# Decoder kernel, fp8 attention stage: the next x is transposed in another PSUM bank, and two norms stand one step later

## The chip, the cores and the metric

The kernel runs on one NeuronCore of a Trainium2 chip. The metric is the time on the device for one execution, in microseconds. Five engines run their own queues in order and meet at semaphores: TensorE (PE; PEld is its weight load), VectorE (DVE), ScalarE (ACT), GpSimd (POOL) and SyncE (SP), which issues the DMAs.

## The reference

A decoder of two layers over x of 16 sequences x 128 tokens x 256 channels. After each block the residual sum is layer-normed. The order is: linear attention, cross-attention, ternary MLP; then a state-space block, the fp8 attention, and a last ternary linear layer. Only the last two are touched here:

```
ln_out = ln(x) * ln_w + ln_b
q, k, v = fp8_linear(ln_out, ...)                # inputs rounded to fp8 values; q: 16 heads, k, v: 4 + 4 groups
q, k = ln(q), ln(k)                              # per head
core = softmax(q k^T / sqrt(d)) v
qx from ln_out; kx, vx from cond @ w_kv_x        # the same attention over the context
cat = fp8(clip([core, xout] / proj_smooth))
y = cat @ wproj * scale
x = layernorm(x + y)                             # norm of the attention, "norm" in the kernel
x = layernorm(x + ternary_linear(x))             # the last norm, "tnorm" in the kernel
```

There are 32 heads in all (16 of each attention) of 128 channels, handled four at a time: 8 units of one batch element.

## The kernel before, in words

The stage is `fp8_attention_and_linear`. Each engine has a function `steps(m, side, attend, front, back, last_linear)` that issues its work for one period m, written out by hand in eight steps j = 0 to 7. Nothing is planned by a scheduler: the order in these functions is the order on the engine. Steps are software-pipelined. In step j of period m:

- TensorE makes the scores of unit j+1 into bank pS (L1920), transposes the probabilities of unit j-1 into bank pP (L1928), multiplies unit j-2 with v into pO (L1938), adds unit j-4 to the projection pY (L1951), transposes the keys of the next batch element into bank pH (L1970), makes a key or value projection of the next element into pJB (L1901 from the context, L1881 from x), transposes the queries of unit j+2 into pH (L2002) and projects those of unit j+3 into pJA (L1881).
- ScalarE does the exponentials of unit j (L2037), copies pP to pT (L2043), copies the keys out of pH (L2028, kT) and the queries out of pH (L2028, qT), then takes the sums of squares of keys or copies v (L2021 k_junk, L2066), and the sums of squares of queries (L2021 q_junk).
- GpSimd turns each sum of squares into a reciprocal root (rs: L1834 and L1837), keys first, then queries, and does two additions of the fp8 rounding of the attention output (ov L1851, cat L1860), and powers for the norms (L107, L1864).
- VectorE takes the maxima of the scores (L2154), scales keys (kn, L2164) and queries (qn, L2170), normalises the probabilities (L2185), and rounds the outputs (L2198 to L2215) and the inputs x (L2129 to L2220, in steps 2 to 6). The norm of the attention has its sum and statistics in step 4 and its apply in step 5 (L112); the last norm has its statistics in step 5 (L98 to L103) and its apply in step 7 (L112).

Keys stand in steps 1, 2, 5 and 6 (`OTHERS`). In step 1 the x of the next batch element is turned too: VectorE makes xn (L2120), TensorE transposes it into pH (L1961), ScalarE scales it into lnT (L2047), and only then the key transposes may use pH. Periods m = 0 to 2 and 16 to 18 are written out singly, m = 4 to 15 are a loop with two periods in its body (`Fori(4, B - 1, 2)`). `attend` holds for m = 1 to 16, `front` (work for the next element) for m = 0 to 15, `back` for m = 2 to 17, `last_linear` for m = 3 to 18.

Of the kernel before, what the change touches and what calls it, by code (L numbers as in the profile page):

```python
# [22 lines left out]
ACT = mybir.ActivationFunctionType  # L23
# [1659 lines left out]
def fp8_attention_and_linear(nc, env, dram, out, ctx, spare):  # L1683
# [147 lines left out]
    def gpsimd(pool):  # L1831
        def rstd(sems, cols, j, count):
            pool.wait_ge(sems["squared"], count)
            pool.tensor_tensor(rs[:, j % 2, cols], ms[:, j % 2, cols], env.eps5w[:, cols], ALU.add)\  # L1834
                .then_inc(sems["eps"], 1)
            pool.wait_ge(sems["eps"], count)
            pool.tensor_tensor(rs[:, j % 2, cols], rs[:, j % 2, cols], env.mhalf[:, cols], ALU.pow)\  # L1837
                .then_inc(sems["rstd"], 1)

        def steps(m, side, attend, front, back, last_linear):  # L1840
            there = presence(attend, front, back)
            for j in range(UNITS):

                if front and j > 0 and OTHERS[j - 1][0] == "k":
                    rstd(kk, slice(HG, 2 * HG), j, at(m + 1, OTHERS[j - 1][1], 4))
                if there(j + 2):
                    rstd(q, slice(0, HG), j, at(m, j + 2))
                if there(j - 3):
                    i = (j - 3) % 2
                    pool.wait_ge(a["om"], at(m, j - 3))  # L1850
                    pool.tensor_tensor(ov[:, i], ob[:, i], om[:, i], ALU.add).then_inc(a["added"], 1)  # L1851
                if front and 2 < j < 7:
                    st = STREAMS[j - 3]
                    pool.wait_ge(sx["xm_done"], at(m + 1, j - 3, 4))
                    pool.tensor_tensor(xv[:, st], xb[:, st], xm[:, st], ALU.add).then_inc(sx["x_added"], 1)
                if attend and not back and j == 3:
                    pool.wait_ge(wp_low, UNITS)
                if there(j - 3):
                    pool.wait_ge(a["added"], at(m, j - 3))
                    pool.tensor_tensor(cat[:, 4 * ((j - 3) % UNITS):4 * ((j - 3) % UNITS) + 4, :], ov[:, i],  # L1860
                                       om[:, i], ALU.subtract).then_inc(a["cat"], 1)
                if front and j == 0:
                    pool.wait_ge(s["eps0_done"], at(m + 1, 0, 1))
                    pool.tensor_tensor(rs0[:], mv0[:, 1:2], env.mhalf[:, 0:1], ALU.pow)\  # L1864
                        .then_inc(s["rs0_done"], 1)
                if back and j == 4:
                    norm.pool_rstd(pool, m - 1, 0)
                if last_linear and j == 6:
                    tnorm.pool_rstd(pool, m - 2, 0)

        env.ssm_stage.left(pool)
        pool.wait_ge(env.fa_ready, 1)
        sequences(pool, steps)

    def tensor(pe):
# [33 lines left out]
        def steps(m, side, attend, front, back, last_linear):  # L1909
            there = presence(attend, front, back)  # L1910
            for j in range(UNITS):
# [12 lines left out]
                if there(j - 1):  # L1924
                    pe.wait_ge(a["p_done"], at(m, j - 1))
                    pe.wait_ge(a["pT_in"], at(m, j - 1) - 1)
                    for i in range(HG):
                        last = pe.transpose(pP[:, i * P:(i + 1) * P], pr[:, (j - 1) % 2, i, :], env.ident[:])  # L1928
                    last.then_inc(a["pT_ps"], 1)
# [24 lines left out]
                    if n == UNITS - 1:  # L1954
                        last.then_inc(s["y_ps"], 1)

                if front and j == 1:
                    pe.wait_ge(s["xn_done"], at(m + 1, 0, 1))
                    pe.wait_ge(q["T_in"], at(m, j + 1))
                    for k in range(KT):  # L1960
                        last = pe.transpose(pH[:, k * P:(k + 1) * P], xn[:, k * P:(k + 1) * P], env.ident[:])  # L1961
                    last.then_inc(s["xn_ps"], 1)
                if keys:
                    n = OTHERS[j - 1][1]
                    pe.wait_ge(kk["scaled"], at(m + 1, n, 4))
                    pe.wait_ge(q["T_in"], at(m, j + 1))
                    if j == 1:
                        pe.wait_ge(s["lnT_in"], at(m + 1, 0, 1))
                    for i in range(HG):
                        last = pe.transpose(pH[:, i * P:(i + 1) * P], kn[:, i, :], env.ident[:])  # L1970
                    last.then_inc(kk["T_ps"], 1)
# [16 lines left out]
                    last.then_inc(t["y_ps"], 1)  # L1988
                if front:
                    other(m + 1, 1 - side, *OTHERS[j])  # L1990
                if there(j + 2):
                    n = (j + 2) % UNITS
                    pe.wait_ge(q["scaled"], at(m, j + 2))
                    pe.wait_ge(q["T_in"], at(m, j + 1))
                    if keys:
                        pe.wait_ge(kk["T_in"], at(m + 1, OTHERS[j - 1][1], 4))
                    if last_linear and j == 3:
                        pe.wait_ge(t["xqT_in"], now(m - 2, 0))
                    if last_linear and j == 4:
                        pe.wait_ge(tnorm.summed, now(m - 2, 0))  # L2000
                    for i in range(HG):
                        last = pe.transpose(pH[:, i * P:(i + 1) * P], qn[:, n % 2, i, :], env.ident[:])  # L2002
                    last.then_inc(q["T_ps"], 1)
# [13 lines left out]
    def scalar(act):  # L2017
# [13 lines left out]
        def steps(m, side, attend, front, back, last_linear):  # L2031
            there = presence(attend, front, back)
            for j in range(UNITS):
                if there(j):
                    act.wait_ge(a["bias"], at(m, j))
                    for i in range(HG):
                        last = act.activation(four(pS[j % 2])[:, i, :], four(pS[j % 2])[:, i, :], ACT.Exp,  # L2037
                                              bias=nb[:, j % 2, i:i + 1],
                                              accum_out=rsum[:, j % 2, i:i + 1])
                    last.then_inc(a["exp"], 1)  # L2040
                if there(j - 1):
                    act.wait_ge(a["pT_ps"], at(m, j - 1))
                    act.activation(pT[:, (j - 1) % 2], four(pP), ACT.Copy).then_inc(a["pT_in"], 1)  # L2043
                if front and j == 1:
                    act.wait_ge(s["xn_ps"], at(m + 1, 0, 1))
                    for k in range(KT):
                        last = act.activation(lnT[:, k, :], pH[:, k * P:(k + 1) * P], ACT.Identity,  # L2047
                                              bias=vec[:, k, 1:2], scale=vec[:, k, 0:1])
                    last.then_inc(s["lnT_in"], 1)
                if front and j > 0 and OTHERS[j - 1][0] == "k":  # L2050
                    n = OTHERS[j - 1][1]
                    head_in(kk, kT[:, 1 - side, n // 2, 4 * (n % 2):4 * (n % 2) + 4, :],
                            6 if n < 2 else 2, m + 1, n, 4)
                if last_linear and j == 3:
                    act.wait_ge(t["xqT_ps"], now(m - 2, 0))
                    act.activation(txqT[:], pH[:, :].bitcast(BF16)[:, 0:D], ACT.Copy).then_inc(t["xqT_in"], 1)
                if there(j + 2):
                    n = (j + 2) % UNITS
                    head_in(q, qT[:, n % 2], 0 if n < 4 else 4, m, j + 2, UNITS)
                if front:  # L2060
                    kind, n = OTHERS[j]
                    if kind == "k":
                        square(kk, pJB, k_junk, ms[:, (j + 1) % 2, HG:2 * HG], m + 1, n, 4)
                    else:
                        act.wait_ge(v_ps, at(m + 1, n, 4))
                        act.activation(v[:, 1 - side, n // 2, (n % 2) * 512:(n % 2 + 1) * 512], pJB[:, :],  # L2066
                                       ACT.Copy).then_inc(v_in, 1)
                if not attend and front:
                    act.wait_ge(wp_in[j % 2], 16 * (j // 2 + 1))
                    act.activation(w_proj[:, 0, 4 * j:4 * j + 4, :], wp_raw[:, j % 2], ACT.Copy)\  # L2070
                        .then_inc(wp_high, 1)
                if there(j + 3):
                    square(q, pJA, q_junk, ms[:, (j + 1) % 2, 0:HG], m, j + 3, UNITS)
# [5 lines left out]
    def vector(dve):  # L2079
# [63 lines left out]
        def steps(m, side, attend, front, back, last_linear):  # L2143
            there = presence(attend, front, back)
            for j in range(UNITS):
# [76 lines left out]
                if not attend and front:  # L2222
                    dve.wait_ge(wp_high, j + 1)
                    dve.tensor_tensor(w_proj[:, 1, 4 * j:4 * j + 4, :], wp_raw[:, j % 2],
                                      w_proj[:, 0, 4 * j:4 * j + 4, :], ALU.subtract).then_inc(wp_low, 1)
                if back and j == 5:
                    norm.vector_apply(dve, m - 1, 0)
                if last_linear and j == 5:
                    tnorm.vector_stats(dve, m - 2, 0)
                if last_linear and j == 7:  # L2230
                    tnorm.vector_apply(dve, m - 2, 0)
# [201 lines left out]
```

## Time and profile before

| | |
|---|---|
| median of 3 runs | 2268.47 us (2267.84 to 2269.28) |
| the profiled execution | 2267.87 us, its span 2265.9 us, mean TensorE clock 0.971 of full speed |
| busy over the span | PE 2043.1 us (90%), DVE 1676.3 (74%), ACT 1332.4 (59%), POOL 1258.8 (56%) |
| chain that ended last | PE 62%, DVE 16%, ACT 10%, issue 7%, POOL 4% |
| periods m = 4 to 14 of this stage | 583.93 us for 11, from the xn transposes of one to those of the next, at full clock |

Busy time is an average over six stages. The stage of the change begins at about 1356 us. A period is found in the timeline by the transposes of xn (L1961), once in each. Times in the rows below are microseconds from the start of the span.

### The profile page before, as it was taken

The page shows a single profiled execution, that of the slowest core. Times are in us where ns is not written, and L with a number is a line of the kernel's source. Part 1 is how long each engine was busy: PE and PEld are TensorE (multiplying, and loading weights), DVE is VectorE, ACT ScalarE, POOL GpSimd, SP SyncE. Part 2 cuts the span into 40 slices and gives each one's busy share as a digit, 9 for nine tenths or more (in the row PEclk, how much of TensorE's full clock was granted, in tenths as well). Part 3 has the DMA queues.
Part 4 walks back from the last instruction along what each step waited for, and adds up shares of the span by engine and source line. Part 5 has one row for each costly group of instructions (what it writes and reads, how often), then busy time and mean ns, then how long its engine had stood idle before and what let it go on. Part 6 is the DMA issues. An engine that isn't in the chain of part 4 may idle for free.

```text
span 2265.9 us, 35512 instructions
## 1 busy us (share of the span) xinstructions
PE 2043.1 (90%) x10014; PEld 1339.2 (59%) x10116; DVE 1676.3 (74%) x3833; ACT 1332.4 (59%) x5022; POOL 1258.8 (56%) x1508
## 2 busy tenths in 40 slices
PE   7889999999999997888889875999999999999996
PEld 5546665666666665555555542666666666666664
DVE  7755676676666777888887864678888888877886
ACT  3655666666666665333333315777777777777773
POOL 0153444544444532566666652676767777776775
PEclk9989999999999999999999987999999999999998
DMA  6000000000000002000000002000000000000000
GB/s 216 1 19 3 3 4 2 5 2 2 2 2 5 0 32 114 1 19 19 19 19 10 1 24 58 4 3 6 6 9 5 6 5 6 5 5 8 3 3 8
DMA packets 30093, 37.61 MB, mean 17 GB/s; under 512 B 3328, under 2 KB 24320, under 8 KB 29312
## 3 DMA queue, kind: packets, MB, share of 16 engines
q1 hardware_dynamic: 29952, 36.11, 4.8%
q8 instruction: 42, 0.69, 0.1%
q14 instruction: 99, 0.81, 0.1%
HBM read 34.00 MB, written 2.10 MB: 16 GB/s over the span
## 4 chain that ended last, share of the span: by engine, by line
PE 62%; DVE 16%; ACT 10%; issue 7%; POOL 4%; DMA 0%; DVEq 0%; SPq 0%; POOLq 0%; ACTq 0%
PE xa_pJB L736 5%; PE xa_pS L755 5%; PE fa_pJB L1901 5%; PE xa_pO L829 5%; PE xa_pY L859 5%; PE xa_pJA L736 4%; PE fa_pS L1920 4%; PE ssm_pX L1404 3%; PE fa_pY L1951 3%; PE fa_pO L1938 3%; PE fa_pJA L1881 3%; PE ssm_pL L1398 3%; PE fa_pH L2002 2%; DVE ssm_y L1665 2%; PE fa_pJB L1881 2%
## 5 line engine op out<-in xcount | busy, mean ns | idle before, releaser
L1346 POOL TENSOR_TENSOR ssm_y<-ssm_y,ssm_term 128x512 f32<-128x512 f32 x112 | 141.9, 1267 | 129.5 <-DVE ssm_term L1612 127.4
L1837 POOL TENSOR_TENSOR fa_rs<-fa_rs,all_minus_half 128x4 f32<-128x4 f32 x192 | 198.2, 1032 | 15.1
L2028 ACT ACTIVATE fa_qT<-fa_pH,all_fa_head_vec 128x512 f32<-128x512 f32 x128 | 99.6, 778 | 173.6 <-PE fa_pH L2002 173.6
L2037 ACT ACTIVATE fa_pS<-fa_pS,fa_nb 128x128 f32<-128x128 f32 x512 | 183.1, 393 | 6.9 <-issue 6.5
L1834 POOL TENSOR_TENSOR fa_rs<-fa_ms,all_eps5w 128x4 f32<-128x4 f32 x192 | 43.7, 228 | 242.1 <-ACT fa_q_junk L2021 132.4
L1920 PEld LDWEIGHTS fa_pS<-fa_kT,fa_qT 128*128 128x128 f32 x1024 | 124.0, 191 | 65.3 <-ACT fa_qT L2028 58.4
L1398 PE MATMUL ssm_pL<-ssm_xd,ssm_cb 128*128 128x512 f32 x224 | 122.3, 643 | 44.3 <-DVE ssm_term L1612 40.5
L1860 POOL TENSOR_TENSOR fa_cat<-fa_ov,fa_om 128x512 bf16<-128x512 f32 x128 | 153.7, 1201 | 5.3
L682 POOL TENSOR_TENSOR xa_rs<-xa_ms,all_eps 128x4 f32<-128x4 f32 (+1 forms) x65 | 13.1, 202 | 258.1 <-ACT xa_junk L904 258.1
L1920 PE MATMUL fa_pS<-fa_kT,fa_qT 128*128 128x128 f32 x1024 | 148.1, 288 | 2.8 <-ACT fa_qT L2028 0.9
L1851 POOL TENSOR_TENSOR fa_ov<-fa_ob,fa_om 128x512 f32<-128x512 bf16 x128 | 147.8, 1154 | 4.7 <-DVE fa_om L2215 4.7
L755 PE MATMUL xa_pS<-all_shared_weights,xa_qT 128*128 128x256 f32 x512 | 125.8, 387 | 23.4 <-ACT all_shared_weights L935 17.5
L2170 DVE TENSOR_TENSOR fa_qn<-fa_pJA,fa_rs 128x512 f32<-128x512 f32 x128 | 88.5, 691 | 77.3 <-POOL fa_rs L1837 77.2
L920 ACT ACTIVATE xa_pr<-xa_pS,xa_nb,xa_rs 128x256 f32<-128x256 f32 x256 | 140.9, 566 | 0.2
L2154 DVE TENSOR_REDUCE fa_nb<-fa_pS 128x4 f32<-128x512 f32 x128 | 88.0, 688 | 69.5 <-PE fa_pS L1920 54.7
L1951 PE MATMUL fa_pY<-all_shared_weights,fa_cat 128*128 128x256 bf16 x1024 | 134.0, 274 | 4.0 <-POOL fa_cat L1860 4.0
L2021 ACT ACTIVATE fa_q_junk<-fa_pJA 128x128 bf16<-128x128 f32 x512 | 136.2, 301 | 0.4
L1404 PE MATMUL ssm_pX<-ssm_w_tap,ssm_xT 128*128 128x512 f32 x256 | 135.6, 647 | 0.0
L2037 ACT ACTIVATION_READ_ACCUMULATOR fa_pS<-fa_pS,fa_nb 128x1 f32 x512 | 133.3, 260 | 0.0
L1938 PE MATMUL fa_pO<-fa_pT,fa_v 128*128 128x256 f32 x512 | 131.9, 380 | 1.4 <-DVE fa_ob L2198 1.4
L1901 PE MATMUL fa_pJB<-all_shared_weights,fa_ctxT 128*128 128x512 f32 x256 | 127.7, 623 | 5.5 <-DMA fa_ctxT<-in_ctxT 4.8
L755 PEld LDWEIGHTS xa_pS<-all_shared_weights,xa_qT 128*128 128x128 f32 x512 | 93.1, 190 | 58.7 <-issue 41.1
(330 smaller groups left out, 5942.1 us busy)
## 6 DMA issues: line engine op xcount, KB each, us to landing
all_shared_weights<-in_fa_w SPq DMA_DIRECT2D x12, 512.0 KB, 3.7
fa_cat<-in_fa_wproj SPq DMA_DIRECT2D x8, 512.0 KB, 3.8
all_shared_weights<-in_xa_wq SPq DMA_DIRECT2D x1, 2048.0 KB, 13.8
xa_wo<-in_xa_wo SPq DMA_DIRECT2D x1, 2048.0 KB, 18.0
xa_ctxT<-in_ctxT SPq DMA_DIRECT2D x16, 128.0 KB, 2.1
all_shared_weights<-in_fa_wkvx SPq DMA_DIRECT2D x1, 2048.0 KB, 10.0
fa_ctxT<-in_ctxT SPq DMA_DIRECT2D x16, 128.0 KB, 2.1
out_x<-all_X SPq DMA_DIRECT2D x16, 128.0 KB, 1.7
```

What stands on the lines that cost most here:

```text
L736: last = pe.matmul(bank[:, :], lhs[k], w[:, k, at0:at0 + 512], start=(k == 0), stop=(k == KT - 1))
L755: last = pe.matmul(pS[b][:, (h % 2) * NK:(h % 2 + 1) * NK], qT[:, n % 2, h, :], kT[:, to, :, n, :], start=True, stop=True)
L1398: pe.matmul(pL[in_turn(side, l)][:, :], cb[:, side, l, :], xd[:, side, l, :], start=True, stop=True).then_inc(level_ps, 1)
L1404: return pe.matmul(pX[:, :], xT[:, k, t:t + P], w_tap[:, t, k, 0:HID], start=(n == 0), stop=(n == TAPS * KT - 1))
L1837: pool.tensor_tensor(rs[:, j % 2, cols], rs[:, j % 2, cols], env.mhalf[:, cols], ALU.pow)\
L1851: pool.tensor_tensor(ov[:, i], ob[:, i], om[:, i], ALU.add).then_inc(a["added"], 1)
L1860: pool.tensor_tensor(cat[:, 4 * ((j - 3) % UNITS):4 * ((j - 3) % UNITS) + 4, :], ov[:, i], om[:, i], ALU.subtract).then_inc(a["cat"], 1)
L1901: last = pe.matmul(pJB[:, :], ctxT[:, side, k, :], w_kvx[:, k, c * 512:(c + 1) * 512], start=(k == 0), stop=(k == KT - 1))
L1920: last = pe.matmul(pS[n % 2][:, i * P:(i + 1) * P], qT[:, n % 2, i, :], kT[:, to, 1 if n < 4 else 0, (4 * (n % 4) + i) // 2, :], start=Tru ...
L1938: last = pe.matmul(pO[:, 2 * i * P:(2 * i + 2) * P], v[:, to, 1 if n < 4 else 0, g * HD:(g + 1) * HD], pT[:, n % 2, 2 * i:2 * i + 2, :], s ...
L1951: last = pe.matmul(pY[:, 0:D], cat[:, hd, :], w_proj[:, part, hd, :], start=(n == 0 and i == 0), stop=(n == UNITS - 1 and i == 2 * HG - 1))
L2037: last = act.activation(four(pS[j % 2])[:, i, :], four(pS[j % 2])[:, i, :], ACT.Exp, bias=nb[:, j % 2, i:i + 1], accum_out=rsum[:, j % 2, ...
```

## The change

In step 1, the transposes of the next x move behind the key transposes and the projection L1901, and go into bank pP (that of the probabilities) instead of pH. ScalarE makes lnT from pP, now behind the copy of the queries. TensorE waits for lnT before the next transposes of the probabilities, in step 2. On VectorE, the apply of the attention's norm and the statistics of the last norm move from step 5 to step 6. On GpSimd, the power for the last norm moves from the end of step 6 into step 7, behind the queries' pair and ahead of ov and cat.

```diff
 gpsimd, steps:
                 if there(j + 2):
                     rstd(q, slice(0, HG), j, at(m, j + 2))
+                if last_linear and j == 7:
+                    tnorm.pool_rstd(pool, m - 2, 0)
...
                 if back and j == 4:
                     norm.pool_rstd(pool, m - 1, 0)
-                if last_linear and j == 6:
-                    tnorm.pool_rstd(pool, m - 2, 0)
 tensor, steps:
                     pe.wait_ge(a["pT_in"], at(m, j - 1) - 1)
+                    if front and j == 2:
+                        pe.wait_ge(s["lnT_in"], at(m + 1, 0, 1))
                     for i in range(HG):
                         last = pe.transpose(pP[:, i * P:(i + 1) * P], pr[:, (j - 1) % 2, i, :], env.ident[:])
...
-                if front and j == 1:
-                    pe.wait_ge(s["xn_done"], at(m + 1, 0, 1))
-                    pe.wait_ge(q["T_in"], at(m, j + 1))
-                    for k in range(KT):
-                        last = pe.transpose(pH[:, k * P:(k + 1) * P], xn[:, k * P:(k + 1) * P], env.ident[:])
-                    last.then_inc(s["xn_ps"], 1)
                 if keys:
                     n = OTHERS[j - 1][1]
                     pe.wait_ge(kk["scaled"], at(m + 1, n, 4))
                     pe.wait_ge(q["T_in"], at(m, j + 1))
-                    if j == 1:
-                        pe.wait_ge(s["lnT_in"], at(m + 1, 0, 1))
...
                 if front:
                     other(m + 1, 1 - side, *OTHERS[j])
+                if front and j == 1:
+                    pe.wait_ge(s["xn_done"], at(m + 1, 0, 1))
+                    if attend:
+                        pe.wait_ge(a["pT_in"], at(m, 0))
+                    for k in range(KT):
+                        last = pe.transpose(pP[:, k * P:(k + 1) * P], xn[:, k * P:(k + 1) * P], env.ident[:])
+                    last.then_inc(s["xn_ps"], 1)
                 if there(j + 2):
 scalar, steps:
-                if front and j == 1:
-                    act.wait_ge(s["xn_ps"], at(m + 1, 0, 1))
-                    for k in range(KT):
-                        last = act.activation(lnT[:, k, :], pH[:, k * P:(k + 1) * P], ACT.Identity,
-                                              bias=vec[:, k, 1:2], scale=vec[:, k, 0:1])
-                    last.then_inc(s["lnT_in"], 1)
                 (copy of the keys)
                 if there(j + 2):
                     n = (j + 2) % UNITS
                     head_in(q, qT[:, n % 2], 0 if n < 4 else 4, m, j + 2, UNITS)
+                if front and j == 1:
+                    act.wait_ge(s["xn_ps"], at(m + 1, 0, 1))
+                    for k in range(KT):
+                        last = act.activation(lnT[:, k, :], pP[:, k * P:(k + 1) * P], ACT.Identity,
+                                              bias=vec[:, k, 1:2], scale=vec[:, k, 0:1])
+                    last.then_inc(s["lnT_in"], 1)
 vector, steps:
-                if back and j == 5:
+                if back and j == 6:
                     norm.vector_apply(dve, m - 1, 0)
-                if last_linear and j == 5:
+                if last_linear and j == 6:
                     tnorm.vector_stats(dve, m - 2, 0)
                 if last_linear and j == 7:
                     tnorm.vector_apply(dve, m - 2, 0)
```

## Rows read from the trace of the kernel before

**Rows 1.** Windows view: us of the window, then busy us of each engine.

```profile
1837.78:1890.83 53.05, 50.59 (x307) 35.32 (x311) 42.31 (x112) 39.89 (x190) 37.62 (x48) 1.00 0.02 6
```

**Rows 2.** Waits of PE, 1572 to 2156 us: total us, times, longest.

```profile
PE fa_pH L1970 <- ACT fa_lnT L2047: 12.3, 11, 1.1
PE fa_pH L1970 <- DVE fa_kn L2164: 8.3, 22, 0.5
```

**Rows 3.** Timeline of step 1: start us, us, engine, line; in brackets idle before.

```profile
1837.07 0.69 DVE L2164 TENSOR_TENSOR fa_kn<-fa_pJB,fa_rs 128x512 f32<-128x512 f32 x1
...
1837.78 0.38 PE L1961 MATMUL fa_pH<-all_ident,fa_xn 128*128 128x128 f32 x2
...
1838.23 0.90 ACT L2047 ACTIVATE fa_lnT<-fa_pH,all_fa_vec 128x128 f32<-128x128 f32 x2
...
1839.28 0.63 PE L1970 MATMUL fa_pH<-all_ident,fa_kn 128*128 128x128 f32 x4 [1.12 <-ACT fa_lnT L2047]
...
1839.74 1.88 PE L1901 MATMUL fa_pJB<-all_shared_weights,fa_ctxT 128*128 128x512 f32 x4
...
1841.46 0.60 PE L2002 MATMUL fa_pH<-all_ident,fa_qn 128*128 128x128 f32 x4
...
1842.78 0.27 ACT L2021 ACTIVATE fa_k_junk<-fa_pJB 128x128 bf16<-128x128 f32 x1
```

**Rows 4.** Timeline of step 2, TensorE and VectorE.

```profile
1843.93 0.60 PE L1928 MATMUL fa_pP<-all_ident,fa_pr 128*128 128x128 f32 x4
...
1845.31 0.69 DVE L2164 TENSOR_TENSOR fa_kn<-fa_pJB,fa_rs 128x512 f32<-128x512 f32 x1 [0.29 <-POOL fa_rs L1837]
...
1846.10 0.62 PE L1970 MATMUL fa_pH<-all_ident,fa_kn 128*128 128x128 f32 x4
```

**Rows 5.** Timeline, end of step 5 and begin of step 6.

```profile
1870.07 0.40 DVE L112 TENSOR_SCALAR all_X<-fa_res,fa_mean_var,fa_rstd 128x256 f32 x1
...
1870.28 1.06 POOL L1837 TENSOR_TENSOR fa_rs<-fa_rs,all_minus_half 128x4 f32<-128x4 f32 x1
...
1870.96 1.04 PE L1951 MATMUL fa_pY<-all_shared_weights,fa_cat 128*128 128x256 bf16 x8
...
1871.19 0.68 DVE L2154 TENSOR_REDUCE fa_nb<-fa_pS 128x4 f32<-128x512 f32 x1
...
1871.79 0.68 DVE L2164 TENSOR_TENSOR fa_kn<-fa_pJB,fa_rs 128x512 f32<-128x512 f32 x1
...
1872.52 0.66 PE L1970 MATMUL fa_pH<-all_ident,fa_kn 128*128 128x128 f32 x4 [0.52 <-DVE fa_kn L2164]
```

**Rows 6.** Timeline, end of step 6 and step 7.

```profile
1876.19 0.42 DVE L2220 TENSOR_TENSOR fa_xq<-fa_xv,fa_xm 128x256 bf16<-128x256 f32 x1
...
1877.19 0.20 POOL L1834 TENSOR_TENSOR fa_rs<-fa_ms,all_eps5w 128x4 f32<-128x4 f32 x1 [1.16 <-ACT fa_q_junk L2021]
...
1878.51 0.69 DVE L2170 TENSOR_TENSOR fa_qn<-fa_pJA,fa_rs 128x512 f32<-128x512 f32 x1 [0.98 <-POOL fa_rs L1837]
...
1879.68 0.60 PE L2002 MATMUL fa_pH<-all_ident,fa_qn 128*128 128x128 f32 x4
...
1879.68 1.16 POOL L1860 TENSOR_TENSOR fa_cat<-fa_ov,fa_om 128x512 bf16<-128x512 f32 x1
```

**Rows 7.** Timeline behind the turn of the loop: steps 0 and 1, m = 10.

```profile
1883.44 1.04 PE L1951 MATMUL fa_pY<-all_shared_weights,fa_cat 128*128 128x256 bf16 x8
...
1884.34 0.69 DVE L2154 TENSOR_REDUCE fa_nb<-fa_pS 128x4 f32<-128x512 f32 x1 [2.36 <-issue]
...
1890.40 0.69 DVE L2164 TENSOR_TENSOR fa_kn<-fa_pJB,fa_rs 128x512 f32<-128x512 f32 x1
...
1892.34 0.63 PE L1970 MATMUL fa_pH<-all_ident,fa_kn 128*128 128x128 f32 x4 [1.12 <-ACT fa_lnT L2047]
```

**Rows 8.** Source view of L112: duration ns min/median/max.

```profile
L112 DVE TENSOR_SCALAR all_X<-ssm_res,ssm_mean_var,ssm_rstd x16: 400/1982/3692, 977.7 to 1353.3; 128x256 f32<-128x256 f32 x16
...
L112 DVE TENSOR_SCALAR all_X<-fa_res,fa_mean_var,fa_rstd x16: 399/400/414, 1499.0 to 2253.1; 128x256 f32 x12, 128x256 f32<-128x256 f32 x4
```

## The prediction

> **What bounds the kernel now.** I read three views. The change touches only the last of the kernel's stages, so the page's averages say little, and I first cut that stage into its periods. A period is one batch element, eight steps j = 0 to 7. In the windows view the one from 1837.78 is 53.05 us long, and TensorE has matmul records over 50.59 us of it [rows 1]. So the stage is bound by TensorE and by the few places where TensorE waits. The list of waits names two kinds in 584 us [rows 2]: the key transposes (L1970) waited 11 times, once a period, for ScalarE's fa_lnT (12.3 us), and 22 times, twice a period, for VectorE's fa_kn (8.3 us). The change aims at one wait of the first kind (step 1) and at one of the second (step 6). Last, the timelines of those steps say what stands behind each.
>
> **Part 1: the transposes of the next x.** In step 1 TensorE transposes xn at 1837.78, ScalarE turns it into lnT at 1838.23 (0.90 us for two), and only then, at 1839.28, can the key transposes start, since both use the bank pH [rows 3]. The keys themselves were ready long before: kn starts at 1837.07 and lasts 0.69, so 1837.76. In the new order the key transposes come first, at about 1837.80, which is 1.48 us earlier. The two xn transposes are not gone: they stand behind the projection L1901, in the bank pP. Four transposes hold TensorE's queue for 0.46 us (L1970 to L1901), two for 0.22 by my halving. So the query transposes (L2002) start 1.48 - 0.22 = 1.26 us earlier, at 1840.20 instead of 1841.46. Their other conditions are met: pP is copied out ahead of lnT on ScalarE (lnT started at 1838.23), long before xn is transposed at about 1839.98, and the keys' own copy would run in that time too.
>
> Now what is late next. ScalarE used to do lnT inside TensorE's wait; now lnT stands behind the copy qT and ahead of the key squares (k_junk). The squares used to start at 1842.78 [rows 3], right behind qT, which follows the query transposes; with all of that 1.26 us earlier lnT starts at 1841.52. It holds ScalarE for 0.68 (two pitches of 0.34: 0.90 less the second's own 0.56) to 0.80 us (0.10 of the 0.90 overlapping what follows); I take 0.74. The squares thus start at 1842.26: earlier in time than 1842.78 by 0.52, but TensorE came 1.26 earlier, so they are 0.74 late against TensorE. Behind them hangs a chain: squares, GpSimd's rs pair, VectorE's kn, key transposes of step 2. In the trace kn of step 2 starts at 1845.31 and ends at 1846.00, and the transposes start at 1846.10, a row without an idle time before it: TensorE was just free [rows 4]. A release by VectorE takes about 0.05, so the slack is 0.05 us. So TensorE will wait 0.74 - 0.05 = 0.69 us there, a new wait in place of the old one, and what is left of part 1 is 1.26 - 0.69 = 0.57 us a period. Bounds: if the lateness were hidden, 1.26; if each lnT held ScalarE for its full 0.556, 1.11 - 0.05 = 1.06 comes back and 0.20 is left. I stay at 0.57, since both the pitch and the slack are read from rows.
>
> The added wait on lnT ahead of the transposes of the probabilities in step 2 has pO, pY and the keys queued behind it. lnT ends at 1841.52 + 0.90 = 1842.42, a release took 0.15 at most (1839.13 to 1839.28), so 1842.57; TensorE arrives at 1843.93 - 1.26 = 1842.67 [rows 4]. It costs nothing, and a small overrun would be swallowed by the 0.69. VectorE's first use of lnT is later still.
>
> Fifteen periods have this step beside attention (m = 1 to 15): 15 x 0.57 = 8.6 us. In the first (m = 0) there is no attention; the old wait goes and the squares come later, as above. I take nothing there, between half a microsecond either way.
>
> **Part 2: the norms on VectorE.** At the end of step 5 stand the apply of one norm and the statistics of the other, 1870.07 to 1871.19, or 1.12 us; only then come the maxima for step 6 (1871.19), kn (1871.79) and the key transposes, 1872.52, where TensorE was free at 1870.96 + 0.87 = 1871.83 [rows 5]. With the 1.12 us gone VectorE could start kn at 1870.67, but GpSimd's power for it runs 1870.28 to 1871.34. So kn moves to 1871.38 and the transposes to 1872.10: 0.42 us gained, of 0.69 lost. Bounds: 0 and 0.69. The wait of step 5 (0.22 in the list, 0.39 by the pitch) has its cause in step 4, from which nothing is taken.
>
> The 1.12 us reappear at the end of step 6. There xq starts at 1876.19, so apply starts at 1876.53, statistics end at 1877.65, the maxima end their slot at 1878.27 and qn goes 1878.27 to 1878.96; TensorE wants it at 1879.68 - 0.42 = 1879.26 [rows 6]. Cover: 0.26 us. The maxima are for a softmax one step on. On GpSimd the 0.6 us power of the last norm goes behind the queries' pair in step 7 and ahead of ov and cat; cat ended at 1880.84, and the projection that reads it started at 1883.44 [rows 6, 7], so 0.6 is covered.
>
> One place returns part of it. When the loop goes round (seen at five even m: 6 to 14), VectorE stands idle for 2.36 us up to 1884.34, with nothing to wait for, and from there runs without pause to kn, 1890.40 [rows 7]. Its step 7 ends only 0.24 us earlier than before (qn 1878.27 against 1878.51), so kn ends 1891.09 - 0.24 = 1890.85, and the key transposes start at 1890.88 rather than 0.42 + 1.48 us earlier than 1892.34. The queries' start then gains 1.46 - 0.22 = 1.24, and step 2 keeps 0.57 of it in total. So in these five periods the 0.42 of the step 6 before them is lost. Of 13 periods with both norms (m = 3 to 15) eight keep it: 8 x 0.42 = 3.4.
>
> **Sum.** 8.6 + 3.4 = 12.0 us. The profiled execution took 2267.87 us (span 2265.9), so 2255.9; the median of the runs, 2268.47, is 0.60 above that execution, so 2256.5. The end of the kernel (m = 16 on) has the same VectorE work in the same queue, which bounds it there: nothing, within half a microsecond.
>
> **A rule against the change.** L112, the apply of a norm, takes 0.40 us in this stage and had a median of 1.98 and a maximum of 3.69 us in the stage before [rows 8]. That GpSimd held it there is my inference. The Trainium skill ("SBUF — State Buffer", Who interferes with whom) says that the shared port pair is an exclusive lock and the second to issue fully blocks; these durations agree with it but do not prove it. By that rule the moved apply can be held, and the last rival below is its price; by the sum above GpSimd is idle at that moment, for 1.16 us up to 1877.19 [rows 6].
>
> **Rivals.**
> (B) ScalarE's lateness does not reach TensorE: part 1 keeps 1.26. 18.9, less 5 x 0.28 where kn itself is late after the loop's turn, plus 3.4: 20.9, so 2247.6. For it: the squares are earlier in absolute time. Against: a slack of 0.05.
> (C) The new wait takes all of it: the lateness is 1.3 us instead of 0.74, as when lnT waits for qT's end and the release adds up. Part 1 gives nothing, 3.4 is left: 2265.1. In effect the change does not do what it says, the wait has only moved a step. For it: a one-for-one chain behind lnT; against: the rows of pitch.
> (D) Slower: in step 6 apply is held by GpSimd. With the 1.98 us of the stage before [rows 8] the tail would be 1.12 - 0.40 + 1.98 = 2.70 us. It decides from 1.12 + 0.26 = 1.38 on; here 1.32 us beyond, each time in 13 periods: +17.2, and 12.0 - 17.2 is 5.2 us slower, 2273.7. Against: 16 of 16 took 0.40 in this stage [rows 8].
>
> **Chances.** The forecast 0.62, B 0.12, C 0.17, D 0.05; 0.04 for something else on the slow side of no change. Alone the forecast reaches 2252 to 2261 (its 0.57 between 0.4 and 0.8, its 0.42 between 0.2 and 0.69). For 8 in 10 the range goes on to C's end and part of the way to B: 2250 to 2265.5. 0.2% is 4.5 us, about what can be told from no change: faster is below 2263.9. That is the forecast, B and a little of C: 0.78; the same 0.15 (most of C); slower 0.07.
>
> **What would show it.** In the changed trace: no wait of L1970 for lnT; in step 1 the key transposes within 0.05 us of pY's end; in step 2 a wait of L1970 for fa_kn of 0.5 to 0.8 us that was not there; in step 6 a wait of 0.1 to 0.3 instead of 0.52, its kn starting on GpSimd's power; periods of 52.0 to 52.5 us, in pairs of 104.5. Wrong would be: a step 2 without a wait (B) or one of 1.2 us and more (C); L2002 of step 7 waiting for fa_qn, or apply longer than 0.5 us (D).

## The result and the profile after

The changed kernel took 2255.81 us (median of 5 runs, 2255.30 to 2259.82), the kernel before 2268.38 us (median of 5, 2266.24 to 2269.28): 12.6 us less. The ratio over all these runs is 0.9949, 95% interval 0.9934 to 0.9964, so the kernel became faster by about half a per cent. Forecast were 2256.5 us and 12.0 us. The profiled span went from 2265.9 to 2253.9 us, 12.0 us less.

The windows view of two periods, from one pair of xn transposes to the next (columns as in [rows 1]):

```profile
1779.54:1831.56 52.02, 50.68 (x308) 35.38 (x311) 43.01 (x113) 39.78 (x187) 37.55 (x48) 1.00 0.02 6
1831.56:1884.56 53.00, 50.96 (x307) 35.30 (x311) 43.05 (x114) 39.89 (x187) 37.95 (x48) 1.00 0.02 6
```

The first period is 52.02 us, against 52.99 for the same one before (1784.79 to 1837.78, by the same transposes). The second is 53.00 against 53.05 [rows 1], as if nothing had been gained: it is one in which the loop goes round, that is, in which the engines branch back to the start of the loop's body. The waits of TensorE in 1572 to 2150 us:

```profile
PE fa_pH L1964 <- DVE fa_kn L2165: 8.3, 24, 0.5
PE fa_pH L2003 <- DVE fa_qn L2171: 2.5, 5, 0.7
```

The wait for lnT [rows 2] is gone. That for kn has the same sum as before, 8.3 us, but it is not the same wait: it left step 6 and came up in step 2. And there is a second kind, five times, for the queries, in step 0 behind each turn of the loop. The list of the kernel before has a third row of this kind, which [rows 2] do not show:

```profile
PE fa_pH L2002 <- DVE fa_qn L2170: 0.4, 2, 0.2
```

It stands in step 0 of m = 6 and m = 14. So TensorE had nothing to spare there even before, in two of five turns. (What is left of the wait in step 6, 0.10 us, is too short for these lists.)

Steps 1 and 2 in the timeline (the lines answer to [rows 3] and [rows 4]; L1964 is the key transposes, L1990 those of xn, L2058 is lnT):

```profile
1828.43 1.04 PE L1953 MATMUL fa_pY<-all_shared_weights,fa_cat 128*128 128x256 bf16 x8
...
1828.59 0.69 DVE L2165 TENSOR_TENSOR fa_kn<-fa_pJB,fa_rs 128x512 f32<-128x512 f32 x1
...
1829.34 0.66 PE L1964 MATMUL fa_pH<-all_ident,fa_kn 128*128 128x128 f32 x4
...
1829.84 1.88 PE L1901 MATMUL fa_pJB<-all_shared_weights,fa_ctxT 128*128 128x512 f32 x4
...
1831.56 0.38 PE L1990 MATMUL fa_pP<-all_ident,fa_xn 128*128 128x128 f32 x2
...
1831.77 0.60 PE L2003 MATMUL fa_pH<-all_ident,fa_qn 128*128 128x128 f32 x4
...
1833.09 0.80 ACT L2058 ACTIVATE fa_lnT<-fa_pP,all_fa_vec 128x128 f32<-128x128 f32 x2
...
1833.78 0.28 ACT L2022 ACTIVATE fa_k_junk<-fa_pJB 128x128 bf16<-128x128 f32 x1
...
1836.33 0.69 DVE L2165 TENSOR_TENSOR fa_kn<-fa_pJB,fa_rs 128x512 f32<-128x512 f32 x1 [0.98 <-POOL fa_rs L1837]
...
1837.07 0.66 PE L1964 MATMUL fa_pH<-all_ident,fa_kn 128*128 128x128 f32 x4 [0.50 <-DVE fa_kn L2165]
```

The keys follow pY at once (1829.34 against 1828.43 + 0.87 = 1829.30). lnT holds ScalarE from 1833.09 to 1833.78, 0.69 us, and only then do the squares start. Their chain ends in kn, which starts at 1836.33, and TensorE, free since pY's end, waits until 1837.07.

End of step 5 and begin of step 6 (against [rows 5]):

```profile
1861.10 0.68 DVE L2155 TENSOR_REDUCE fa_nb<-fa_pS 128x4 f32<-128x512 f32 x1
1861.31 1.02 POOL L1837 TENSOR_TENSOR fa_rs<-fa_rs,all_minus_half 128x4 f32<-128x4 f32 x1
...
1861.97 1.04 PE L1953 MATMUL fa_pY<-all_shared_weights,fa_cat 128*128 128x256 bf16 x8
...
1862.36 0.69 DVE L2165 TENSOR_TENSOR fa_kn<-fa_pJB,fa_rs 128x512 f32<-128x512 f32 x1 [0.59 <-POOL fa_rs L1837]
...
1863.11 0.66 PE L1964 MATMUL fa_pH<-all_ident,fa_kn 128*128 128x128 f32 x4
```

VectorE is early now and is idle for 0.59 us until GpSimd's power is done, as forecast; TensorE starts the keys 0.27 us after pY frees it (1861.97 + 0.87 = 1862.84) instead of 0.69.

A table of step lengths (from one pS of TensorE to the next, read from the timelines) separates the terms. "Turn" is the mean over m = 6, 8, 10, 12, 14, the periods behind a turn of the loop; "plain" is m = 5.

| kernel | step 1 plain | step 1 turn | step 2 | step 6 | step 0 plain | step 0 turn | last pS to end |
|---|---|---|---|---|---|---|---|
| before | 8.32 | 8.32 | 6.81 | 6.97 | 6.44 | 6.66 | 35.4 |
| changed | 7.11 | 7.38 | 7.51 | 6.54 | 6.44 | 7.16 | 36.0 |

The other steps of these periods agree within 0.02. The turn is uneven: before, its step 0 took 6.52 to 6.90, since the idle time of VectorE in it was 2.36 to 2.75 us long. Summed over all periods, the changed kernel is shorter by 18.8 us in step 1 and 5.7 in step 6, longer by 10.5 in step 2 and 2.5 in step 0, and shorter by 0.4 in the first period's last step and by 0.1 in all the rest. The end is 0.6 longer. The stage's first pS, with which that last step of m = 0 begins, comes 0.6 earlier (1398.54 against 1399.10). Of this, 0.1 is there when the stage before ends (1353.15 against 1353.29), and 0.4 arises in the earlier steps of m = 0, where the xn transposes were moved too. This makes the 12.0 of the span.

### The profile page after: what moved, and what is told of

Same layout as the page of the kernel before. It is cut to its first block, busy times and chain, and to the rows that moved or that the text cites. A ratio compares the mean times of both kernels' runs of the same rounds, so it can differ in the third digit from the quotient of the medians.

```text
span 2253.9 us, 35511 instructions
## 1 busy us (share of the span) xinstructions
PE 2042.5 (91%) x10014; PEld 1338.0 (59%) x10116; DVE 1681.1 (75%) x3833; ACT 1332.0 (59%) x5022; POOL 1260.3 (56%) x1508
## 4 chain that ended last, share of the span: by engine, by line
PE 60%; DVE 18%; ACT 8%; issue 8%; POOL 4%; DMA 0%; DVEq 0%; SPq 0%; POOLq 0%; ACTq 0%
PE xa_pJB L736 5%; PE xa_pS L755 5%; PE xa_pO L829 5%; PE xa_pY L859 5%; PE fa_pJB L1901 5%; PE xa_pJA L736 4%; PE ssm_pX L1404 3%; PE fa_pS L1920 3%; PE ssm_pL L1398 3%; PE fa_pY L1953 2%; PE fa_pO L1940 2%; PE fa_pJA L1881 2%; PE fa_pH L2003 2%; DVE ssm_y L1665 2%; POOL fa_rs L1837 2%
## 5 line engine op out<-in xcount | busy, mean ns | idle before, releaser
L1901 PE MATMUL fa_pJB<-all_shared_weights,fa_ctxT 128*128 128x512 f32 x256 | 126.2, 617 | 5.6 <-DMA fa_ctxT<-in_ctxT 4.9
L1881 PE MATMUL fa_pJA<-fa_w_all,fa_xq 128*128 128x512 bf16 x463 | 125.2, 383 | 2.6
```

The lines of the kernel that those rows point to most:

```text
L1881: last = pe.matmul(bank[:, :], xq[:, side, st, k, :], w_all[:, part, k, cols], start=(i == 0), stop=(i == 2 * KT - 1))
L1901: last = pe.matmul(pJB[:, :], ctxT[:, side, k, :], w_kvx[:, k, c * 512:(c + 1) * 512], start=(k == 0), stop=(k == KT - 1))
```

## The experiments

All kernels were timed beside the kernel before on the same chip. Its median was 2267.99 us beside the two kernels with one part alone, the one with lnT early and the one with the power last, and 2267.33 us beside the other four; with 2268.38 above, such medians lie a microsecond apart. In the profiled executions the stages ahead of this one also differ by up to 3.5 us between the kernels, though no edit touches them. So where a difference is small I go by the step lengths.

**One part alone.** The xn transposes in pP with the norms where they were:

```diff
 changed kernel, vector and gpsimd
-                if back and j == 6:
+                if back and j == 5:
                     norm.vector_apply(dve, m - 1, 0)
-                if last_linear and j == 6:
+                if last_linear and j == 5:
                     tnorm.vector_stats(dve, m - 2, 0)
...
-                if last_linear and j == 7:      # ahead of ov and cat
+                if last_linear and j == 6:      # behind cat
                     tnorm.pool_rstd(pool, m - 2, 0)
```

> Part 1 alone: xn transposes in pP behind L1901, norms where they were. Step lengths are from one pS (L1920) to the next; before: step 1 8.32 us, step 2 6.81, step 6 6.98. Theory (the old wait goes, the key squares come 0.7 us late behind lnT, GpSimd's power and kn bound step 6 only in part 2): step 1 7.10, step 2 7.51, step 6 stays 6.98, step 0 after the turn of the loop stays 6.5 and the step 1 after it is 7.38. In all about 9.4 us less than before: 2259. Rival 'the parts need each other' (VectorE's tail in step 5 sets the period): under 3 us less, 2265 or more. Rival 'step 2 hides the squares': step 2 6.81, about 2249.

Measured: 2258.56 us, ratio 0.9957 (0.9943 to 0.9971), 9.4 us less than before. Expected was 2259. Step 1 is 7.10, step 2 7.52, step 6 6.99, step 1 behind the turn 7.38, step 0 there 6.73. The waits of TensorE show keys waiting three times a period, in steps 2, 5 and 6:

```profile
PE fa_pH L1964 <- DVE fa_kn L2165: 14.0, 34, 0.5
```

And the norms alone, with xn still in pH:

```diff
 kernel before, vector and gpsimd
-                if back and j == 5:
+                if back and j == 6:
                     norm.vector_apply(dve, m - 1, 0)
-                if last_linear and j == 5:
+                if last_linear and j == 6:
                     tnorm.vector_stats(dve, m - 2, 0)
...
-                if last_linear and j == 6:      # behind cat
+                if last_linear and j == 7:      # ahead of ov and cat
                     tnorm.pool_rstd(pool, m - 2, 0)
```

> Part 2 alone: apply and statistics in step 6, the power of the last norm in step 7, xn still in pH. Theory: step 1 8.32 and step 2 6.81 as before; step 6 6.54 instead of 6.98 in 13 periods (5.7 us), of which the turn of the loop takes back some 0.5 in each of five step 0, and the end of the kernel 0.6: about 2.6 us less, 2265.8. Rival 'the tail costs nothing in step 6': all 5.7 stay, 2262.7, step 0 after the turn as before. Rival 'the tail is as dear in step 6 as it was in step 5': 2268.4.

Measured: 2266.56 us, ratio 0.9991 (0.9982 to 1.0000). That is 1.4 us less than before, where 2.6 was expected (2265.8 us on the record), and the interval reaches 1: the time alone does not tell it from no change. In the profile step 6 is 6.54, step 1 8.31, step 2 6.81, and step 0 behind the turn 7.20. So the second part gains 5.8 us in step 6 and gives 2.7 back, nearly all at the turns, and 0.6 at the end. By these steps both rivals fall: the moved work is neither free nor as dear as before. The two parts add to the whole: from the stage's first pS on, the profiles give 8.5 us for the first part, 2.9 for the second and 11.4 for both. In the medians they are 9.4 and 1.4 against 12.6.

**Where the wait of step 2 comes from.** Two kernels pull on it from both sides. In one the xn transposes stand between the two halves of L1901, and lnT between ScalarE's copies of keys and queries:

```diff
 changed kernel, tensor: other()
                 for k in range(KT):
                     last = pe.matmul(pJB[:, :], ctxT[:, side, k, :], ...)
+                    if k == 0 and between:
+                        between()              # the two xn transposes of step 1
 scalar
                 (copy of the keys)
+                if front and j == 1:
+                    (wait xn_ps, the two lnT activations, lnT_in)
                 if there(j + 2):
                     head_in(q, ...)            # copy of the queries
-                if front and j == 1:
-                    (wait xn_ps, the two lnT activations, lnT_in)
```

> The changed kernel with the two xn transposes between the two halves of the projection L1901 and lnT on ScalarE between the copies kT and qT, where ScalarE was idle for 1.59 us. Theory (the wait in step 2 is the squares' lateness behind lnT and nothing else): step 1 stays 7.10, step 2 falls from 7.51 to 6.81 in 15 periods: 10.5 us less than the changed kernel, 2245.3. Rival 'step 2 waits for the bank pP or for its new semaphore wait': step 2 stays at 7.5, 2255.8.

Measured: 2246.66 us, ratio 0.9904 (0.9890 to 0.9918), 9.2 us less than the changed kernel, where 10.5 was expected; from the first pS on, the profiles differ by 10.8. Step 2 is 6.81 and step 1 stays 7.11. The timeline of its steps 1 and 2:

```profile
1825.57 0.78 ACT L2032 ACTIVATE fa_kT<-fa_pH,all_fa_head_vec 128x512 f32<-128x512 f32 x1
...
1826.23 0.38 PE L1916 MATMUL fa_pP<-all_ident,fa_xn 128*128 128x128 f32 x2
...
1826.65 0.80 ACT L2058 ACTIVATE fa_lnT<-fa_pP,all_fa_vec 128x128 f32<-128x128 f32 x2 [0.30 <-PE fa_pP L1916]
1827.95 0.78 ACT L2032 ACTIVATE fa_qT<-fa_pH,all_fa_head_vec 128x512 f32<-128x512 f32 x1 [0.49 <-PE fa_pH L2006]
...
1831.90 0.42 PEld L1974 LDWEIGHTS fa_pH<-all_ident,fa_kn 128*128 128x128 f32 x4
1831.95 0.62 PE L1974 MATMUL fa_pH<-all_ident,fa_kn 128*128 128x128 f32 x4
```

lnT has idle time on both sides (0.30 before it, 0.49 behind it), so it delays nothing behind it on ScalarE, and the keys of step 2 start with no idle time. This alone does not clear the bank pP and the new wait on lnT: lnT is done earlier here too, so those conditions are met earlier as well.

The other kernel leaves them as they are and doubles the suspected cost:

```diff
 changed kernel, scalar, behind lnT
                     last.then_inc(s["lnT_in"], 1)
+                    for k in range(KT):
+                        act.activation(lnT_more[:, k, :], env.ident[:, :], ACT.Identity,
+                                       bias=vec[:, k, 1:2], scale=vec[:, k, 0:1])
```

> The changed kernel with ScalarE's lnT pair doubled by two more activations of 128x128 between lnT and the key squares (they write a tile that nobody reads; lnT itself is released as before). Theory (each us that ScalarE is late with the squares is a us of TensorE in step 2): step 2 grows by the pair's slot, 0.69 us, from 7.51 to 8.20, in 15 periods: 10.4 us more than the changed kernel, 2266.2. Rival 'step 2 is longer for another reason, as the new semaphore wait or the bank pP': step 2 stays 7.51, 2255.8.

Measured: 2268.74 us, ratio 1.0004 (0.9995 to 1.0013), where 2266.2 was expected: the whole gain is gone. Step 2 is 8.26, 0.75 more than in the changed kernel. The expectation had 0.69, the slot of a pair that reads PSUM; this pair reads SBUF and holds ScalarE for 0.77 us, from 1842.09 to the squares at 1842.86:

```profile
1842.09 0.87 ACT L2063 ACTIVATE fa_lnT_more<-all_ident,all_fa_vec 128x128 bf16<-128x128 f32 x2
1842.86 0.27 ACT L2023 ACTIVATE fa_k_junk<-fa_pJB 128x128 bf16<-128x128 f32 x1
```

Of the other steps, the last of the first period is 0.5 longer and single steps 0 behind a turn moved by up to 0.2; the rest did not move by 0.1. The wait grew as it should:

```profile
PE fa_pH L1965 <- DVE fa_kn L2169: 16.6, 24, 1.3
```

ScalarE came 0.77 us later with the squares of step 2, and TensorE lost 0.75. Since lnT was released as before and pP is free as before, neither is the cause of the wait in step 2.

**What the turn of the loop takes.** The forecast had 0.42 us lost at each of five turns; step 0 and step 1 there lost 0.5 and 0.27. Timeline of the changed kernel around the turn to m = 10 (against [rows 6] and [rows 7]):

```profile
1869.05 0.56 POOL L107 TENSOR_TENSOR tl_rstd<-tl_mean_var,all_minus_half 128x1 f32<-128x1 f32 x1
1869.24 0.68 DVE L2171 TENSOR_TENSOR fa_qn<-fa_pJA,fa_rs 128x512 f32<-128x512 f32 x1
...
1870.81 1.16 POOL L1862 TENSOR_TENSOR fa_cat<-fa_ov,fa_om 128x512 bf16<-128x512 f32 x1
1871.36 0.76 DVE L2205 TENSOR_SCALAR fa_ob<-fa_ob 128x512 bf16<-128x512 bf16 x1
...
1872.69 0.41 DVE L112 TENSOR_SCALAR all_X<-tl_res,tl_mean_var,tl_rstd 128x256 f32 x1
...
1875.53 0.69 DVE L2155 TENSOR_REDUCE fa_nb<-fa_pS 128x4 f32<-128x512 f32 x1 [2.43 <-issue]
...
1877.26 0.66 PE L2003 MATMUL fa_pH<-all_ident,fa_qn 128*128 128x128 f32 x4 [0.48 <-DVE fa_qn L2171]
...
1881.61 0.68 DVE L2165 TENSOR_TENSOR fa_kn<-fa_pJB,fa_rs 128x512 f32<-128x512 f32 x1
...
1882.34 0.42 PEld L1964 LDWEIGHTS fa_pH<-all_ident,fa_kn 128*128 128x128 f32 x4 [0.43 <-DVE fa_kn L2165]
```

In step 7 qn starts 3.01 us behind TensorE's pS, where it was 2.87 before: 0.14 later against TensorE, 0.18 forecast (0.42 less 0.24). New is the length of the clip L2205 in this step: 0.76 us, where in step 7 of the kernel before it took 0.35:

```profile
1880.64 0.35 DVE L2204 TENSOR_SCALAR fa_ob<-fa_ob 128x512 bf16<-128x512 bf16 x1
```

It starts at 1871.36 inside cat, which runs to 1871.97, and ends at 1872.12. cat is there because the power L107 stands ahead of ov and cat now. So VectorE ends step 7 0.55 us later against TensorE than before (0.14 by qn, 0.41 by the clip), is idle for its 2.4 us from there, and TensorE waits for qn in step 0 and for kn in step 1. I tested this by moving the power to the end of step 7:

```diff
 changed kernel, gpsimd
-                if last_linear and j == 7:      # ahead of ov and cat
-                    tnorm.pool_rstd(pool, m - 2, 0)
...
+                if last_linear and j == 7:      # behind cat
+                    tnorm.pool_rstd(pool, m - 2, 0)
```

> The changed kernel with GpSimd's power of the last norm (L107) at the end of step 7, behind ov and cat instead of ahead of them. Theory (the power pushed cat by 0.55 us onto VectorE's clip, which took 0.76 us in step 7 against 0.35 before, so VectorE reaches the loop's turn 0.56 late, and TensorE waits for qn and kn after it): the clip back to about 0.35, five turns 0.4 us shorter each, 2 us in all, and up to 0.6 at the end: 2253.2 to 2253.8. Rival 'the loop's turn costs what it costs, or only the moved maxima count (0.15 us)': no change, 2255.8.

Measured: 2253.70 us, ratio 0.9936 (0.9922 to 0.9950), 2.1 us less than the changed kernel and inside the 2253.2 to 2253.8 that was expected. The clip is short again, and the power runs where GpSimd was idle:

```profile
1870.43 1.16 POOL L1860 TENSOR_TENSOR fa_cat<-fa_ov,fa_om 128x512 bf16<-128x512 f32 x1
...
1871.51 0.29 DVE L2205 TENSOR_SCALAR fa_ob<-fa_ob 128x512 bf16<-128x512 bf16 x1
1871.55 0.68 POOL L107 TENSOR_TENSOR tl_rstd<-tl_mean_var,all_minus_half 128x1 f32<-128x1 f32 x1
```

Step 0 behind the turn is 6.85 instead of 7.16, which is 1.5 us over the five, and the end of the kernel 35.0 us instead of 36.0. Step 1 behind the turn stays at 7.38, as it did with the xn transposes alone, where neither the norms nor the power had moved: it has another bound, VectorE's unbroken run from its idle time to kn. The 0.27 was hidden as long as TensorE waited for lnT in that step. Writing the loop out takes VectorE's idle time away and tests this:

```diff
-        with eng.Fori(4, B - 1, 2) as m:
+        for m in range(4, B - 1, 2):
             steps(m, 0, True, True, True, True)
             steps(m + 1, 1, True, True, True, True)
```

> The changed kernel with the 12 periods of the loop written out (no branch). Theory (the loop's turn stops VectorE for 2.4 us and ScalarE for 1.2, and TensorE now runs into that): in the five places step 0 falls from 7.1 to 7.3 to 6.44 and step 1 from 7.38 to 7.10, 1.0 us each: 5 us less than the changed kernel, 2250.8. Rival 'instructions come in as slowly without a branch': the same idle time elsewhere, 2255.8 or more.

Measured: 2251.69 us, ratio 0.9930 (0.9917 to 0.9944): 4.1 us less than the changed kernel by the medians, where 5 was expected. From the first pS on, the profiles differ by 6.2. All periods are alike now: step 0 6.36, step 1 7.11. Step 0 fell by 0.08 also where the loop does not turn (6.44 before); why is open. The five waits for qn are gone from the list, where this one kind is left:

```profile
PE fa_pH L1964 <- DVE fa_kn L2165: 8.5, 23, 0.5
```

**The mends together.** Both edits at once on the changed kernel, the one between the halves of L1901 and the one of the power:

```diff
 changed kernel
+                    if k == 0 and between:     # tensor: xn between the halves
+                        between()
...
-                if front and j == 1:           # scalar: lnT ahead of head_in(q)
...
-                if last_linear and j == 7:      # gpsimd: ahead of ov and cat
+                if last_linear and j == 7:      # gpsimd: behind cat
```

> Both mends together on the changed kernel: xn transposes between the halves of L1901 with lnT between kT and qT, and the last norm's power at the end of step 7. Theory: the two gains add, since one is in step 2 and the other at the loop's turn: 2246.7 less 2.1 = 2244.6; step 2 6.81, step 0 after the turn 6.85. Rival 'one hides the other': 2246.7.

Measured: 2243.20 us, ratio 0.9897 (0.9882 to 0.9913), where 2244.6 was expected; step 2 6.81, step 0 behind the turn 6.74. The two gains add. That step 0 is 0.12 shorter than with the power alone; VectorE's idle time at the turns averaged 2.50 us in this execution and 2.61 in that one, which accounts for it.

And the same with the loop written out, by the edit of the two lines shown above:

> e6 with the loop written out. Theory: of the turns 0.4 + 0.28 us each are left in e6, so 3.4 us less than e6: 2241.2. Rival as for the unrolled kernel: 2244.6 or more.

Measured: 2239.90 us, ratio 0.9881 (0.9866 to 0.9896), where 2241.2 was expected: 27.4 us less than the kernel before and 15.9 less than the changed one. It is the fastest of all. What is left in a period is the waits of TensorE for kn in steps 5 and 6.

## Why the prediction was right

- Part 1, the first gain: 1.26 us a period was forecast; step 1 fell from 8.32 to 7.11, 1.21. The keys start 1.46 us earlier within the step, not 1.48, and their four transposes hold the queue for 0.50 us (1829.34 to 1829.84) instead of 0.46. In m = 1, which I priced like the others, the gain was 2.97, since lnT had cost 2.04 us of waiting there, and in m = 2 and 3 1.36 and 1.28. Over 15 periods that is 1.9 us more and 0.6 less than the sum had.
- Part 1, the new wait: 0.69 forecast, 0.70 measured in every one of the 15 periods. The agreement to a hundredth is luck: lnT's slot was 0.69, where I took 0.74; less the slack of 0.05 the keys of step 2 start 0.66 us late (3.83 us behind their pS against 3.17), and their transposes then hold the queue for 0.50 us instead of 0.45, which no term had. The mechanism is not luck. It is shown by the two kernels that take the lateness away and that double it.
- The wait on lnT ahead of the probabilities cost nothing: it heads no row of the list.
- The first period: nothing within half a microsecond was forecast. 0.8 was gained, 0.4 ahead of the first pS and 0.4 in the step behind it, so this lies outside what was said. With the pair on ScalarE doubled, the second 0.4 turned into a loss of 0.1; the first period was not looked into further.
- Part 2 in step 6: 0.42 forecast, 0.44 measured, and bound by GpSimd's power as said.
- The turns: this is the term that was mis-sized. 5 x 0.42 = 2.1 us was forecast, step 0 gave 2.5 and step 1 1.4, together 3.9. I had said that the power ahead of ov and cat is covered, and looked only at who reads cat. VectorE's clip beside cat was missing. With the power last, step 0 gives 0.9 and step 1 the same 1.4, together 2.3, so the clip is some 1.5 of the 1.8 that were missing. I had also read two kinds of waits in the list, where there are three; the third, for qn, said that lateness in step 0 of a turn reaches TensorE.
- The end of the kernel: nothing within half a microsecond was forecast, 0.6 was lost. It is 35.0 us in all three kernels with the power last and 36.0 in all five with the norms moved and the power first, against 35.4 before, so the power's place decides it.
- So the sum of 12.0 came out, but with 1.3 in step 1, 0.8 in the first period, 0.3 in step 6 and 0.2 of small differences on one side, and 1.8 at the turns, 0.6 at the end and 0.1 in step 2 on the other, which happened to cancel. A pair of periods was forecast at 104.5 us and is 105.0.

The rivals: B (step 2 hides the squares) and C (the wait has only moved) both fail on the 0.70; C's picture was more than half true, since 10.5 of the 18.8 us gained in step 1 did only move. D (apply held by GpSimd in step 6) did not occur, apply took 0.41 us in all 16 places; but the same kind of contention struck one step on, at the clip. I had cited the rule of the Trainium skill ("SBUF — State Buffer", Who interferes with whom) that the second to issue blocks until the first is done; the clip, ending 0.15 us after cat, agrees with it.

## What to carry to other kernels

When a wait is removed by moving work behind another instruction, count what that work now stands in front of: here lnT went from a place where ScalarE idled to the head of a chain with 0.05 us of slack by the rows of the kernel before, and over half of the gain came back as a wait one step on. The same work placed into idle time of its engine kept all of it (2246.7 us against 2255.8). And when an operation on GpSimd moves, look at which VectorE operation the ones behind it come to stand beside, not only at who reads them.

## What the runs showed of the hardware

The turn of this loop, whose body is two periods of some 53 us, leaves VectorE idle for 2.4 to 2.7 us and ScalarE for 1.2 to 1.5 us with no semaphore behind it. The idle time starts when VectorE's own work ends (at the turn to m = 10 that is 0.55 us later against TensorE in the changed kernel, and the idle time is 2.43 us instead of 2.36), so whatever lets VectorE end later passes through it; with the loop written out it is gone and the kernel 4.1 us faster. TensorE shows no such idle time at the turns; it loses time only where it waits for what VectorE makes late. Why the turn costs this is not shown by any run.

In the changed kernel a clip of 128x512 in bf16 took 0.28 to 0.29 us on VectorE in each of the 70 places where no GpSimd instruction ran beside it. In the 37 places where it began with about 0.2 us or more left of a GpSimd addition (ov or cat), it took 0.34 to 1.16 us and ended 0.14 to 0.15 us after the addition, each time.

Two ScalarE activations of 128x128 in fp32 out of PSUM have a record of 0.80 us but hold the queue for 0.69. The two that read SBUF and write bf16 have a record of 0.87 us and hold it for 0.77.
